# The beginning of a fused adaLN block: filler matmuls, later weight loads, setup moved behind the first scores

## The reference

```python
mod = (_silu(L0_c) @ L0_wmod).reshape(4, 6, 1, -1)
sa, ca, ga, sb, cb, gb = (mod[:, i] for i in range(6))   # ga, gb: sign kept, size at least 0.25
h = _layernorm(x) * (1 + ca) + sa
q, k, v = split(h @ qkv_w.T)                             # 16 heads of 16
x = x + ga * (softmax(q @ k.T * 0.25) @ v @ proj_w.T + proj_b)
h = _layernorm(x) * (1 + cb) + sb
# 8 experts (auto-encoders): the one with the least reconstruction error on h picks the adapter
base = h @ W_base + b_base
recon = relu(h @ W_enc[n] + b_enc[n]) @ W_dec[n] + b_dec[n]
top1 = argmin(mean((recon - h) ** 2))                    # for each batch
x = x + gb * (base + relu(h @ W_down[top1] + ..) @ W_up[top1] + ..)
```

## Time and profile before

| | before |
|---|---|
| median of three runs | 1005.38 us (1002.44 to 1008.56) |
| the profiled execution, its own time | 1006.59 us |
| its span in the trace | 1004.7 us |
| PE busy | 962.5 us, 96% |
| DVE busy | 800.2 us, 80% |
| ACT busy | 660.5 us, 66% |
| POOL busy | 333.5 us, 33% |
| mean granted clock of TensorE | 0.981 |

### The profile page before, as it was taken

One profiled execution on the slowest core, in us unless ns is written; L12 is line 12 of the kernel. 1 busy time (PEld: TensorE's weight loads), 2 busy tenths in 40 slices (PEclk: granted clock), 3 DMA queues, 4 the chain that ended last, 5 costly groups with the idle time before them and its releaser, 6 DMA issues.

```text
span 1004.7 us, 16505 instructions
## 1 busy us (share of the span) xinstructions
PE 962.5 (96%) x5794; PEld 477.9 (48%) x5794; DVE 800.2 (80%) x1631; ACT 660.5 (66%) x1295; POOL 333.5 (33%) x443
## 2 busy tenths in 40 slices
PE   6989999999899999999999999999999999999998
PEld 4444344434344445455454445445454455544476
DVE  4889988999587887878788787787788788888455
ACT  2148787887576777666668676766657767565831
POOL 4210234124265343111447433311247413116320
PEclk9889999999899999999999999999999999998999
DMA  7850061243450503253242511415324411132001
...
DMA packets 47890, 66.93 MB, mean 67 GB/s; under 512 B 12139, under 2 KB 32112, under 8 KB 47796
## 3 DMA queue, kind: packets, MB, share of 16 engines
q1 hardware_dynamic: 46572, 65.00, 30.2%
...
...
## 4 chain that ended last, share of the span: by engine, by line
PE 76%; DVE 8%; ACT 5%; DMA 3%; POOL 3%; SPq 3%; issue 2%; ACTq 0%; DVEq 0%; POOLq 0%
PE pE L816 25%; PE pO L816 21%; PE pX L816 18%; PE pM L816 11%; DVE mx L1302 4%; SPq L1888 2%; ACT P L1123 2%; DMA QO<-lo 1%; ACT h1T L1164 1%; DVE h2f L1463 1%; ACT h2f L1214 1%; DMA xin<-in_x 1%; DVE junk L1439 1%; DMA P<-in_wmod 0%; DMA orow<-outs 0%
## 5 line engine op out<-in xcount | busy, mean ns | idle before, releaser
L1302 DVE TENSOR_REDUCE mx<-pM 128x1 f32<-128x512 f32 x1006 | 630.9, 683 | 116.5 <-PE pM L816 110.4
L1123 ACT ACTIVATE P<-pE 128x512 f32<-128x512 f32 x996 | 525.7, 600 | 183.0 <-PE pE L816 180.1
L816 PE MATMUL pM<-KO,QO 48*128 48x512 f32 x1006 | 368.2, 455 | 9.9 <-DVE mx L1302 6.0
L816 PE MATMUL pE<-QO,KO 50*128 50x512 f32 x996 | 348.9, 440 | 12.4 <-ACT h1T L1164 5.0
L816 PEld LDWEIGHTS pE<-QO,KO 50*128 50x128 f32 x996 | 165.6, 188 | 239.0 <-issue 128.9
L816 PE MATMUL pO<-P,V 128*17 128x512 f32 x2048 | 262.9, 609 | 5.1 <-ACT P L1123 5.1
L816 PEld LDWEIGHTS pM<-KO,QO 48*128 48x128 f32 x1006 | 164.8, 188 | 39.4 <-DVE mx L1302 27.4
L816 PEld LDWEIGHTS pO<-P,V 128*17 128x17 f32 x2048 | 40.6, 96 | 104.9 <-issue 90.5
L1713 POOL CAST mh<-mxc 128x16 fp32r<-128x16 f32 x32 | 6.5, 203 | 181.2 <-DVE mxc L1311 180.9
L1772 POOL TENSOR_TENSOR Hs<-h2f,Hs 128x512 fp32r<-128x512 f32 x28 | 35.6, 1282 | 73.6 <-ACT Hs L1244 58.4
L816 PE MATMUL pX<-h1T,wqkv_s 128*128 128x512 f32 x112 | 59.2, 642 | 0.4 <-DVE acc L1497 0.3
...
## 6 DMA issues: line engine op xcount, KB each, us to landing
...
```

Of the source, the lines that this page charges most:

```text
L816: return e.matmul(o, lhsT, rhs, start=start, stop=stop)
L1123: e.activation(P[:, u % 3, j, :], bank(s), ACT.Exp).then_inc(*empties(s))
L1302: e.tensor_reduce(mx[:, hq % 2, k:k + 1, kh], bank(s), AX.X, ALU.max, negate=True).then_inc(*empties(s))
```

## The change

Five things, all of the beginning.

1. `("warm", k)`: 5, 1 and 2 matmuls of 256 columns on the tile `osb`, which DVE first sets to zero, into bank pX that nothing reads. The first five stand at the head of the program, the others between the first transposes; two more stand inside `modT`.
2. The loads of wd, wdT and of the 1 MB of wmod leave SP's queue after the six QO copies of half 0 (a new step `weights`).
3. `setupa`, `setupb`, `setupq` and `setupc` move among the 48 M; `be` moves behind the second half's qk; `v` 2 and 3 leave the 48 M and come with the first E (plan, u = 0). `gates` stand 13 steps later, `mturn` 3 earlier, `modT2` at u = 5. The steps beside come after M 1, 5, 9 and so on, rather than after M 3, 7, 11.
4. The semaphores of gi = 0's copies are split by the partitions that they fill, and the first 16 M take heads 0, 0, 0, 0, 2, 2, 2, 2 before 1 and 3, all with the keys of half 0. So the first eight M wait for three copies of QO and three of KO.
5. `NEAR` = 2: for gi = 2 POOL makes hi and lo, where DVE did.

```diff
-NEAR = 3
+NEAR = 2
+WARM = (5, 1, 2)
...
-    at(1, ("modT2",))
+    at(0, ("v", 0, 2), ("v", 0, 3))
+    at(5, ("modT2",))
...
-    out += [("be",), ("ln1n", 0, 3)] + [(("qk", 0, 0, 0), p) for p in range(2)]
+    out = [("warm", 0), ("open",), ("ln1s", 0, 0), ("ln1s", 0, 1), ("ln1n", 0, 0), ("modT",)]
+    out += [("ln1turn", 0, 0), ("warm", 1), ("ln1n", 0, 1), ("ln1turn", 0, 1), ("warm", 2), ("ln1s", 0, 2)]
+    out += [("ln1n", 0, 2), ("ln1s", 0, 3), ("ln1n", 0, 3)] + [(("qk", 0, 0, 0), p) for p in range(2)]
...
-    out += [("ln1turn", 0, 2), ("ln1turn", 0, 3), ("setupa",)] + [(("qk", 0, 0, 1), p) for p in range(2)]
-    out += [("copy", 0, w, i, 1) for i in range(6) for w in (1, 0)] + [("setupb",), ("setupq",)]
+    out += [("ln1turn", 0, 2), ("ln1turn", 0, 3)] + [(("qk", 0, 0, 1), p) for p in range(2)] + [("be",)]
+    out += [("copy", 0, 1, i, 1) for i in range(6)] + [("weights",)] + [("copy", 0, 0, i, 1) for i in range(6)]
...
+    beside = deque([("qk", 0, 1, 0), ("qk", 0, 1, 1), ("setupa",), ("setupb",), ("setupc",)])
+    beside += [("modmm", 1), ("modmm", 2), ("qk", 0, 2, 0), ("qk", 0, 2, 1)] + [("v", 0, 0), ("v", 0, 1)]
     for i in range(LEAD):
-        if i and i % 4 == 0 and beside:
+        if i % 4 == 2 and beside:
...
+            if hq == 0 and jp == 0:
+                return hq, 2 * (r // 4 % 2) + r // 8, r % 4, 0
...
-                        pe.wait_ge(d_op0[0][c], 16 * 6)
-                        pe.wait_ge(d_op0[1][kh], 16 * 6)
+                        pe.wait_ge(d_op0[0][c][j % 2], 16 * 3)
+                        pe.wait_ge(d_op0[1][kh][j % 2], 16 * 3)
...
+                elif kind == "warm":
+                    pe.wait_ge(s_warm, 1)
+                    for k in range(WARM[s[1]]):
+                        mm(pX[:, 0:256], osb[:, 0:128], osb[:, 0:256])
...
+                        if k in (0, 2):
+                            mm(pX[:, 0:256], osb[:, 0:128], osb[:, 0:256])
...
+            e.memset(osb[:, :], 0.0).then_inc(s_warm, 1)
```

More of the change, by code:

```diff
@@ L229, in order @@
 def order():
-    out = [("open",), ("ln1s", 0, 0), ("ln1s", 0, 1), ("ln1n", 0, 0), ("modT",)]
-    out += [("ln1turn", 0, 0), ("ln1n", 0, 1), ("ln1turn", 0, 1), ("ln1s", 0, 2), ("ln1n", 0, 2), ("ln1s", 0, 3)]
-    out += [("be",), ("ln1n", 0, 3)] + [(("qk", 0, 0, 0), p) for p in range(2)]
+    out = [("warm", 0), ("open",), ("ln1s", 0, 0), ("ln1s", 0, 1), ("ln1n", 0, 0), ("modT",)]
+    out += [("ln1turn", 0, 0), ("warm", 1), ("ln1n", 0, 1), ("ln1turn", 0, 1), ("warm", 2), ("ln1s", 0, 2)]
+    out += [("ln1n", 0, 2), ("ln1s", 0, 3), ("ln1n", 0, 3)] + [(("qk", 0, 0, 0), p) for p in range(2)]
     out += [("copy", 0, w, i, 0) for i in range(6) for w in (1, 0)]
-    out += [("ln1turn", 0, 2), ("ln1turn", 0, 3), ("setupa",)] + [(("qk", 0, 0, 1), p) for p in range(2)]
-    out += [("copy", 0, w, i, 1) for i in range(6) for w in (1, 0)] + [("setupb",), ("setupq",)]
-    beside = deque([("qk", 0, 1, 0), ("qk", 0, 1, 1), ("setupc",), ("modmm", 1), ("modmm", 2)])
-    beside += [("v", 0, t) for t in range(4)] + [("qk", 0, 2, 0), ("qk", 0, 2, 1)]
+    out += [("ln1turn", 0, 2), ("ln1turn", 0, 3)] + [(("qk", 0, 0, 1), p) for p in range(2)] + [("be",)]
+    out += [("copy", 0, 1, i, 1) for i in range(6)] + [("weights",)] + [("copy", 0, 0, i, 1) for i in range(6)]
+    beside = deque([("qk", 0, 1, 0), ("qk", 0, 1, 1), ("setupa",), ("setupb",), ("setupc",)])
+    beside += [("modmm", 1), ("modmm", 2), ("qk", 0, 2, 0), ("qk", 0, 2, 1)] + [("v", 0, 0), ("v", 0, 1)]
     for i in range(LEAD):
-        if i and i % 4 == 0 and beside:
+        if i % 4 == 2 and beside:
             s = beside.popleft()
             out += [(s, p) for p in range(PIECES[s[0]])] if s[0] in PIECES else [s]
+            if s == ("setupb",):
+                out.append(("setupq",))
             if s == ("qk", 0, 1, 1):
@@ L248, in order @@
         out.append(("M", i))
-        if 20 <= i < 29:
-            out.append(("gates", i - 20))
+        if 33 <= i < 42:
+            out.append(("gates", i - 33))
         if i == 31:
             out.append(("mmax", 0))
-        if i == 39:
+        if i == 36:
             out.append(("mturn", 0))
+    assert not beside
     due, m = plan(), LEAD
@@ L711, in adaln_block @@
         d_op = [sem(f"d_op{g}") for g in range(4)]
-        d_op0 = [[sem(f"d_opp{w}{half}") for half in range(2)] for w in range(2)]
+        d_op0 = [[[sem(f"d_opp{w}{half}{par}") for par in range(2)] for half in range(2)] for w in range(2)]
         d_m = [[sem(f"d_m{i}{j}") for j in range(4)] for i in range(2)]
@@ L833, in tensor @@
                     else:
-                        pe.wait_ge(d_op0[0][c], 16 * 6)
-                        pe.wait_ge(d_op0[1][0], 16 * 6)
-                        pe.wait_ge(d_op0[1][1], 16 * 6)
+                        for par in range(2):
+                            pe.wait_ge(d_op0[0][c][par], 16 * 3)
+                            pe.wait_ge(d_op0[1][0][par], 16 * 3)
+                            pe.wait_ge(d_op0[1][1][par], 16 * 3)
                     pe.wait_ge(d_m[hq % 2][j], 16 * (hq // 2 + 1))
@@ L1172, in scalar @@
                     if gi == 2:
-                        act.wait_ge(d_op0[0][half], 16 * 6)
-                        act.wait_ge(d_op0[1][half], 16 * 6)
+                        for par in range(2):
+                            act.wait_ge(d_op0[0][half][par], 16 * 3)
+                            act.wait_ge(d_op0[1][half][par], 16 * 3)
                     elif gi > 2:
@@ L1707, in gpsimd @@
                     e.dma_start(*move(0, 1, i, thirds(0, 1), slice(512 * half, 512 * half + 512))).then_inc(
-                        d_op0[1][half], 16)
+                        d_op0[1][half][i // 3], 16)
                 elif kind == "mmax":
```

11 lines of the change are left out of this document (5 added, 6 removed).

## The result

The changed kernel took 1010.97 us (median of 7 runs, 1004.70 to 1014.57) against 1005.38 us before: a ratio of 1.0056, 95% interval 1.0034 to 1.0079. Run again later beside other kernels it gave 1.0028 (1.0006 to 1.0050, 12 runs). It is a little slower, where 7 us less were forecast.

A forecast was written before the change was run, and what follows sets the result against it. PE was taken as full (96% busy) after the beginning, DVE as the bound once M runs. PV 1 9.0 us earlier less 1.5 gave 7.5: 999.1 from the profiled execution, 997.9 from the median, forecast 998.5 us, range 993 to 1005.

The forecast's parts named there:

- Part 1, the first copies, the first M: Beginning: fillers raise the clock, copies start at 16.4, 1.5 us earlier; first maximum at 21.8, 5.8 us earlier.
- rival B: Beginning: clock not risen before the first qk, modT ends at 11.6, copies start at 18.9; total 1001 us; chance 0.10.
- The 48 M: First maximum to end of the 48th: DVE the bound, PE's steps hidden; 35.8 us instead of 37.3, ending at 57.6.
- The start of E: From the 48th maximum to PV 1: v 2 fills the stretch, 6.0 to 6.3 us; PV 1 at 63.8, 9.0 earlier.
- v 3 and modT2 later: Between PVs after PV 1: v 3's later PE work mostly hidden; 1.0 us charged, 0.5 for modT2, 1.5 in all.
- NEAR = 2: Among the 48 M: two lo of gi = 2, 0.75 us each, leave DVE for an idle POOL, 1.5 us less.
- rival A: Between first qk and first M: clock falls again, two qk take 1.8 us more each; total 1002 us; chance 0.17.
- no window at 0.50 before: Sign for the stretch up to PV 1: the granted clock shows no window at 0.50 before PV 1 at 63.8.
- Rival C: DMA queue: 2 MB of loads delay mT's rows past 61.7; E 0 at 64, 3 us slower, 1009; chance 0.07.

The follow-up runs named there:

- a0_again: The changed kernel run once more, nothing altered: ratio 1.0028 to the kernel before; its profiled execution took 1013.34 us.
- c1_setups_ahead: The changed kernel without fillers, with setupa, setupb, setupq, be and the weight loads back where they stood before: ratio 0.9978 to the kernel before, 1002.04 us.
- a1_nofill: The changed kernel without its ten filler matmuls, the memset kept: ratio 1.0008 to the kernel before, 1005.23 us.
- d1_loads_early: The changed kernel without fillers, loads of wd and wdT ahead of all copies, wmod's behind those of half 1: ratio 1.0003 to the kernel before, 1007.15 us.
- c2_vmove: The kernel before with part 4, v 2 and 3 moved behind the first E and modT2 to u = 5: ratio 0.9992, 1003.37 us.
- a2_setupfill: The changed kernel with two filler matmuls of 256 columns inside each of setupa, setupb and setupc: ratio 1.0002 to the kernel before, 1005.55 us.
- c3_near2: The kernel before with part 4 (split semaphores, new order of the first 16 M) and NEAR = 2: ratio 0.9963, 999.86 us.
- b2_split: The kernel before with part 4 alone (split semaphores, new order of the first 16 M): ratio 0.9983, 1004.07 us.
- b1_fill: The kernel before with the ten filler matmuls alone added: ratio 1.0027, 1008.75 us.
- d2_v_first: c3_near2 with v 0 and 1 ahead of modmm 1 and 2, and the gates 8 steps later: ratio 0.9924 to the kernel before, 998.42 us.

## Why the prediction was wrong

By its own steps:

- **Part 1, the first copies, the first M: right in the first trace, in part by luck.** modT ended at 8.55 (forecast 9.1), the copies started at 15.78 (16.4), M 0 at 21.54 (21.2), the first maximum at 22.20 (21.8), 5.4 us earlier than before (5.8). The copies started 0.6 earlier than forecast and then took 5.8 us rather than 4.8, and the two misses nearly cancel. In a0_again's trace the clock rose later, and rival B came in place of this.
- **The 48 M: this is the step that failed.** I wrote that PE's steps beside "are as many as before (eleven), each 2 us or less per four M, and hide under the 2.5 us of four maxima", and forecast 35.8 us on DVE; it was 62.7 - 22.2 = 40.5. DVE's own work was 33.4 us, where the terms give 32.8 - 1.5 + 1.3 = 32.6; its waits were put at 3.2 (4.5 - 1.3) and were 7.1: 3.0 at the first h2h (1.0 forecast), 1.4 around setupb and 2.1 behind setupc (nothing forecast). The step "2 us or less" was setupb with setupq at 3.83 and setupc at 3.78, at the lower level. Even at the upper level a step of 1.98 and the 0.64 that four M take together make 2.6 us, more than 2.5. That DVE alone was the bound was read from the maxima's own chain; the window from M 0 to E 0 before, PE 33.88 of 35.00 us, would have told that PE had no room for what was to hide. The setups stood before where PE had 3.4 us of idle ahead of the copies. c1_setups_ahead against a1_nofill puts their move, with the loads', at 3 us, and d1_loads_early points to the setups; neither is far beyond noise.
- **The start of E: the second failure, as large.** From the 48th maximum to PV 1 I forecast 6.2 us, it took 10.9 (7.9 before). The pieces of v were to "fill that stretch" at 1.0 us each; they ran at 2.07, and DVE waited 1.85 and 1.69 us for PE. The forecast named the window at 0.50 before, and assumed that more work would lift it. In c2_vmove it did not. In a2_setupfill's trace, where the level was the upper one, the stretch took 6.4: the sum was right for a clock that was not granted.
- **v 3 and modT2 later: -1.5 forecast.** From PV 1 to PV 10 the change lost 0.6 (0.8 later at the first, 97.82 against 96.45 at the last).
- **NEAR = 2: right in size**, 1.5 forecast, 1.8 at E 0 in the traces and 2 us by the ratios (c3_near2 against b2_split), the latter within noise.
- **The clock, rival A: half of it.** The second qk was at the upper level (1.96), the one behind M 1 took 3.25, 1.3 more: "no window at 0.50 before" failed from 21.7 us on. The rest of what the clock took came where no rival looked: among the M and behind E 0. The Trainium skill (TensorE: Matmul & The Clock Gate, part 4) says that a transpose doesn't count as busy in the way that a matmul does. The traces don't decide it: behind the same eight transposes the second qk was fast in six traces (1.96 in the changed kernel, 1.95 in d1_loads_early, which has no fillers) and slow in a1_nofill's (3.43), and in b1_fill's it was slow behind the eight and setupa (3.76).
- **Rival B** came in a0_again's trace and in no other of the seven with the ten fillers.
- **Rival C** did not come: in the changed kernel PE had no idle time ahead of E 0, so the rows of mT were there. It came in d2_v_first's trace alone (2.16 us).

The parts by the ratios: split -1.7 us, NEAR = 2 -2, v and modT2 +1 to +1.5, setups and loads +3, fillers +2 to +5. That they add up to the measured +2.8 and +5.6 is no confirmation, since most of them are steps of one chain from the kernel before to the changed one. Measured apart from that chain are the fillers (+2.7 on the kernel before, +4 on the split) and v's move (+0.9 on the split, within noise). Two of the five parts seem to gain, near 4 us together, and three take more than that away.
